# First cross attention: the values product of the second 128 keys as three passes over half-precision splits, with VectorE making the lower split of the turned probabilities

## What is computed

```python
xn = layer_norm(x, g1, b1)                    # context, 257 rows a batch
ln_lat = layer_norm(latents, g2, b2)          # 32 rows a batch
q = ln_lat @ Wq
kv = jnp.concatenate([xn, ln_lat], axis=1) @ Wkv
k, v = jnp.split(kv, 2, axis=-1)              # 16 heads of 64
weight = einsum('bhld,bhnd->bhln', q * scale, k * scale)
weight = softmax(where(full_mask, weight, neg))
out = einsum('bhln,bhnd->bhld', weight, v) @ Wout
```

## Time and profile before

| what | value |
|---|---|
| median of three runs | 2339.83 us |
| the profiled execution's own time | 2338.32 us |
| its span, first to last instruction | 2335.7 us |
| granted TensorE clock, mean of the span | 0.912 |
| PE busy | 1966.3 us, 84% |
| VectorE busy | 1634.2 us, 70% |
| ScalarE busy | 1632.0 us, 70% |
| GpSimd busy | 900.8 us, 39% |

### The profile page before, as it was taken

How to read it: one execution, slowest core, us unless ns; L and a number is a source line. 1 busy time by engine, 2 the same in 40 slices (tenths; PEclk the granted TensorE clock), 3 DMA queues, 4 the chain that set the end, 5 groups by cost and what they waited for, 6 DMA issues and landing times. The chain is left out here.

```text
span 2335.7 us, 56137 instructions
## 1 busy us (share of the span) xinstructions
PE 1966.3 (84%) x15558; PEld 1552.0 (66%) x15558; DVE 1634.2 (70%) x5153; ACT 1632.0 (70%) x4429; POOL 900.8 (39%) x1341
## 2 busy tenths in 40 slices
PE   3799999999999999973430359999999989957997
PEld 3688888888888888851320127777777756625775
DVE  5677777777777777745566738888888878854654
ACT  3588888888888888854365328888888878834553
POOL 2533333333333333303033303333333347733554
PEclk8799999999999999986575669999999999968999
DMA  4211111111111111000000012222222200012322
GB/s 133 68 33 32 32 32 32 32 32 32 32 32 32 32 32 32 19 1 0 0 0 0 0 43 65 66 69 72 63 71 63 67 2 1 1 27 70 93 80 86
DMA packets 124104, 93.87 MB, mean 40 GB/s; under 512 B 14416, under 2 KB 101936, under 8 KB 123904
## 3 DMA queue, kind: packets, MB, share of 16 engines
q1 hardware_dynamic: 122550, 90.88, 14.2%
q10 hardware_dynamic: 1194, 1.58, 0.2%
q0 software_dynamic: 288, 0.56, 0.1%
HBM read 88.26 MB, written 4.72 MB: 40 GB/s over the span
## 5 line engine op out<-in xcount | busy, mean ns | idle before, releaser
L751 ACT ACTIVATE a_prob<-a_neg,a_nmax 128x289 f32<-128x289 f32 x512 | 270.6, 530 | 78.8 <-DVE a_nmax L680 72.9
L1645 ACT ACTIVATE b_prob<-b_neg,b_nmax 128x257 f32<-128x257 f32 x512 | 255.2, 500 | 71.1 <-DVE b_nmax L1592 71.0
L646 POOL TENSOR_TENSOR a_xn<-a_z,g 128x256 f32<-128x256 f32 x128 | 93.2, 728 | 526.3 <-DVE a_z L706 526.3
L808 PE MATMUL a_score<-a_xnT,a_qT 128*128 128x290 f32 x1536 | 274.2, 314 | 1.1 <-DVE a_qT L727 1.1
L836 PE MATMUL a_out<-a_probT,a_xn 128*128 128x256 f32 x1024 | 263.5, 380 | 0.3 <-DVE a_probT L691 0.3
L680 DVE CUSTOM_DVE_ANT_0 a_neg<-a_score,a_bias 128x289 f32<-128x289 f32 x512 | 221.9, 459 | 46.4 <-PE a_score L808 40.7
L808 PEld LDWEIGHTS a_score<-a_xnT,a_qT 128*128 128x128 f32 x1536 | 216.0, 190 | 43.8 <-issue 43.2
L1592 DVE CUSTOM_DVE_ANT_0 b_neg<-b_score,b_bias 128x257 f32<-128x257 f32 x512 | 196.1, 421 | 50.7 <-PE b_score L1688 48.1
L756 ACT ACTIVATE a_prob<-a_prob,a_rinv 128x256 f32<-128x256 f32 x512 | 230.5, 499 | 1.1 <-DVE a_rinv L718 1.0
L836 PEld LDWEIGHTS a_out<-a_probT,a_xn 128*128 128x128 f32 x1024 | 174.8, 191 | 13.7 <-DVE a_probT L691 0.6
L1566 POOL TENSOR_TENSOR b_last_part<-b_v_rows,b_prob 128x128 f32<-128x128 f32 x128 | 52.0, 406 | 317.4 <-ACT b_prob L1645 317.3
(11 more groups left out here) (465 smaller groups left out, 5230.6 us busy)
## 6 DMA issues: line engine op xcount, KB each, us to landing
a_raw<-in_ctx SPq DMA_DIRECT2D x128, 128.0 KB, 3.3
b_raw<-in_ctx SPq DMA_DIRECT2D x128, 128.0 KB, 3.2
m_wide<-expert_weights SPq DMA_DIRECT2D x128, 128.0 KB, 2.9
a_kept<-keep SPq DMA_DIRECT2D x32, 257.0 KB, 3.8
b_kept<-keep SPq DMA_DIRECT2D x32, 257.0 KB, 3.5
b_v_rows<-ctx_tail_values SPq DMA_DIRECT2D x32, 256.0 KB, 3.6
a_tail<-latents_normalised SPq DMA_DIRECT2D x64, 64.0 KB
latents_normalised<-lat_affine SPq DMA_DIRECT2D x8, 256.0 KB, 2.3
```

The costliest lines, as they stand in the source:

```text
L751: nc.scalar.activation(prob[:, par, grp, :], neg[:, grp, :], ACT.Exp, bias=nmax[:, par, grp:grp + 1], scale=-1.0, accum_out=rsum[:, par, g ...
L808: last = nc.tensor.matmul(score_ps[grp % 2][:, 0:even(KEYS0)], qT[:, a, un, bn, 4 * grp:4 * grp + 4, :], xnT[:, c, n, :], start=(p == 0), ...
L1645: nc.scalar.activation(prob[:, n, grp, :], neg[:, par, grp, :], ACT.Exp, bias=nmax[:, par, grp:grp + 1], scale=-1.0, accum_out=rsum[:, n, ...
```

## The change

The second 128 keys' values are taken out of the plain F32 form. `values` is split in `values0` (first 128 keys, as before) and `values1`, which runs three passes of F32R halves for each half of the heads: six F32R instructions of 256 columns where four F32 instructions stood. The halves are made in three places. GpSimd makes those of `xn` (a cast of 128x128 into `xn1[:, n, HI]`, then a subtraction into `xn1[:, n, LO]`). ScalarE's copy L765 writes the upper half of the turned probabilities into `probT1[:, HI, :]` in place of the F32 copy. VectorE subtracts that from the turned probabilities in PSUM and writes `probT1[:, LO, :]`, 128x512 elements, a new instruction between masks 3 and the statistics. TensorE waits for both lower halves ahead of `values1`.

```diff
--- before.py
+++ after.py
@@ -548,6 +548,9 @@
         var, rstd = sb("a_var", [P, 2, 2]), sb("a_rstd", [P, 2, 2])
         z = sb("a_z", [P, 2, 2, D])
         xn = sb("a_xn", [P, 8, 2, D])
+
+        xn1 = sb("a_xn1", [P, 8, 2, D], F32R)
+        probT1 = sb("a_probT1", [P, 2, CH], F32R)
         tail = sb("a_tail", [P, 8, D])
         xnT = sb("a_xnT", [P, 2, 8, even(KEYS0)], F32R)
         kept = sb("a_kept", [P, 2, BPT, N_CTX], BF16)
@@ -575,6 +578,7 @@
         turned, probT_ready = [sem(f"a_turned{n}") for n in range(3)], [sem(f"a_probT_ready{n}") for n in range(3)]
         out_ready, oT_ready, proj_ready, x_added = (sem(f"a_{n}") for n in ("out_ready", "oT_ready", "proj_ready", "x_added"))
         zeroed, tail_prob_ready = sem("a_zeroed"), sem("a_tail_prob_ready")
+        xn1_hi, xn1_ready, probT1_ready = sem("a_xn1_hi"), sem("a_xn1_ready"), sem("a_probT1_ready")
         x_stats_ready = sem("a_x_stats_ready")
         LEAD, LAG = 5, 1
 
@@ -646,6 +650,12 @@
                         nc.gpsimd.tensor_tensor(xn[:, n], z[:, par], spread(k.g1), ALU.mult).then_inc(scaled, 1)
                         pool.wait_ge(scaled, s + 5)
                         nc.gpsimd.tensor_tensor(xn[:, n], xn[:, n], spread(k.b1), ALU.add).then_inc(xn_ready, 1)
+                        pool.wait_ge(xn_ready, s + 5)
+                        if live(g, j, -4):
+                            wait_apart(k, pool, out_ready, s - 3)
+                        nc.gpsimd.tensor_copy(xn1[:, n, HI], xn[:, n, 1]).then_inc(xn1_hi, 1)
+                        pool.wait_ge(xn1_hi, s + 5)
+                        nc.gpsimd.tensor_tensor(xn1[:, n, LO], xn[:, n, 1], xn1[:, n, HI], ALU.subtract).then_inc(xn1_ready, 1)
                     if live(g, j, 5):
                         par = (j + 5) % 2
                         wait_apart(k, pool, mv_ready, s + 6)
@@ -692,6 +702,9 @@
                     if live(g, j, 1):
                         mask(g, j, 2)
                         mask(g, j, 3)
+                    if live(g, j, 0):
+                        dve.wait_ge(probT_ready[1], s + 1)
+                        nc.vector.tensor_tensor(probT1[:, LO, :], turn_ps[1][:], probT1[:, HI, :], ALU.subtract).then_inc(probT1_ready, 1)
                     if live(g, j, 5):
                         n, par = (j + 5) % 8, (j + 5) % 2
                         dve.wait_ge(raw_loaded[n], (g + (j + 5) // 8 + 1) * 16)
@@ -762,7 +775,7 @@
                         exp(g, j, 1)
                     if live(g, j, 0):
                         act.wait_ge(turned[1], s + 1)
-                        nc.scalar.activation(probT[:, 1, :], turn_ps[1][:], ACT.Copy).then_inc(probT_ready[1], 1)
+                        nc.scalar.activation(probT1[:, HI, :], turn_ps[1][:], ACT.Copy).then_inc(probT_ready[1], 1)
                     if live(g, j, 1):
                         exp(g, j, 2)
                         exp(g, j, 3)
@@ -827,14 +840,22 @@
                         last = nc.tensor.transpose(turn_ps[0][:, i * P:(i + 1) * P], prob_tail[:, j % 2, i].rearrange("p f n -> p (f n)"), k.ident[:])
                     last.then_inc(turned[2], 1)
 
-                def values(g, j, kt):
+                def values0(g, j):
                     s = g * 8 + j
-                    pe.wait_ge(probT_ready[kt], s + 1)
-                    if kt == 0:
-                        wait(pe, oT_ready, s)
+                    pe.wait_ge(probT_ready[0], s + 1)
+                    wait(pe, oT_ready, s)
                     for half in range(2):
-                        nc.tensor.matmul(out_ps[:, half, 0:2 * P], xn[:, j, kt, :], probT[:, kt, half * 2 * P:(half + 1) * 2 * P],
-                                         start=(kt == 0), stop=False)
+                        nc.tensor.matmul(out_ps[:, half, 0:2 * P], xn[:, j, 0, :], probT[:, 0, half * 2 * P:(half + 1) * 2 * P],
+                                         start=True, stop=False)
+
+                def values1(g, j):
+                    s = g * 8 + j
+                    pe.wait_ge(xn1_ready, s + 1)
+                    pe.wait_ge(probT1_ready, s + 1)
+                    for a, c in PASSES:
+                        for half in range(2):
+                            nc.tensor.matmul(out_ps[:, half, 0:2 * P], xn1[:, j, a, :], probT1[:, c, half * 2 * P:(half + 1) * 2 * P],
+                                             start=False, stop=False)
 
                 def tail_values(g, j):
                     s = g * 8 + j
@@ -877,7 +898,7 @@
                             last = nc.tensor.matmul(proj_ps, oT[:, h, :], k.U[:, h, :], start=(h == 0), stop=(h == H - 1))
                         last.then_inc(proj_ready, 1)
                     if here:
-                        values(g, j, 0)
+                        values0(g, j)
                         turn_tails(g, j)
                     if live(g, j, 3):
                         n = (j + 3) % 8
@@ -889,7 +910,7 @@
                             last = nc.tensor.transpose(ctx_ps[:, kt * P:(kt + 1) * P], xn[:, n, kt, :], k.ident[:])
                         last.then_inc(ctx_turned, 1)
                     if here:
-                        values(g, j, 1)
+                        values1(g, j)
                         tail_values(g, j)
 
                 run_steps(pe, step, LEAD, LAG)
```

## The result

Four runs of the changed kernel gave 2386.51 to 2390.66 us, with a median of 2388.14; the kernel before gave 2338.88 beside it (four runs, 2337.04 to 2342.24). The ratio is 1.021, with a 95% interval of 1.0192 to 1.0228. The change made the kernel 49 us slower. The forecast was 2393, 54.5 us slower, in a range of 2374 to 2408. The profiled execution took 2386.51 us, its span 2384.7.

What follows compares the result with a forecast made beforehand. A loop through PE, VectorE's reciprocal and ScalarE was taken to bound three of four steps, PE the other. The profiled 2338.32 + 57.3 (subtraction) - 2.8 (shorter product) gave 2392.8, forecast 2393 us, range 2374 to 2408.

Steps and rivals of the forecast that it cites:

- The bound: Of a tile's four steps, one is paced by PE, three by a loop through PE, VectorE's reciprocal and ScalarE.
- The subtraction, 0.61 us in 94 steps: VectorE's new instruction ahead of the reciprocal lengthens the loop in three of four steps: 57.3 us slower.
- The six passes, 0.78 us instead of 0.87: F32R passes on PE replace four F32 instructions, saving 0.09 us in 31 first steps of tiles: 2.8 us gained.
- The sum: Whole kernel: 2338.32 + 57.3 - 2.8 = 2392.8 us, given as 2393.
- What was to cost nothing: ScalarE's copy into F32R, and GpSimd's cast and subtraction of 0.73 us a step, were put at nothing.
- The wait of PE ahead of `tail_values`, put near 1 us: In a tile's second to fourth step PE should wait near 1 us for ScalarE's copy.
- PE as the pace of every step: Rival: VectorE has 0.61 us to spare, only the shorter product counts; 11.4 us less, 2327; chance 0.05.
- That nothing happens: Rival: subtraction slips into VectorE's idle time, shorter product only waits longer on PE; 2338 us; chance 0.04.
- GpSimd against VectorE: Rival: GpSimd's new operations stretch a VectorE instruction on the loop; 9 to 19 us more, 2402 to 2412; chance 0.08.
- The granted clock: Rival: PE's waits lower its clock for a tenth of the stage; up to 94 us more, some 2480; chance 0.05.

Runs made afterwards that it cites:

- e2: Kernel before plus only VectorE's new subtraction, written to a buffer nobody reads, and TensorE's wait for it; 2391.53 us, ratio 1.0231.
- e4: Changed kernel with VectorE's work for later batches moved behind the reciprocal, last keys' scaling and queries' lower half; nothing left out; 2332.62 us, ratio 0.9977 to kernel before.
- e5: Kernel before, F32 products kept, with VectorE's work for later batches moved behind the reciprocal, last keys' scaling and queries' lower half; 2334.56 us, ratio 0.9983.
- e1: Changed kernel without VectorE's new subtraction; its pass reads the upper half again, so six passes remain; 2336.08 us, ratio 0.9988 to kernel before.
- e3: Kernel before plus only GpSimd's new cast and subtraction of 128x128, written to a buffer nobody reads; 2339.29 us, ratio 1.0004.
- e6: Changed kernel with VectorE's subtraction over the first 256 of 512 columns only; other heads' pass reads the upper half; 2362.74 us, ratio 1.0108.

## Why the prediction was right, and where its sizes were off

**The bound.** Right. The loop through PE, VectorE's row up to the reciprocal, ScalarE's scaling and copy, and `tail_values` was read from two distances of 0.04 and 0.06 us. e2 lengthens it by one instruction and pays in full; e4 takes 1.05 us of other work out of it and gets the 0.60 back. What the prediction did not say is that in the kernel before this loop was not the bound alone. The scaling began 514.15 - 513.67 = 0.48 us after the query half, and in e4, where the query half alone holds it, it is 523.87 - 523.39 = 0.48 too. So in this step VectorE's row and ScalarE's own ended together; the fourth step is the same, and only in the third does VectorE's row end last, by 0.1 us (below). That is why 0.61 us more on VectorE's row costs 0.60, while 1.05 us less on it (e5) gives 0.01 in the second and the fourth step.

**The subtraction, 0.61 us in 94 steps.** The mechanism and the price hold: 0.61 from start to start in the timeline, and e1 against the changed kernel gives 7.45 - 6.85 = 0.60 in the second step and 7.04 - 6.44 = 0.60 in the fourth. In the third step it is only 7.03 - 6.52 = 0.51. That step was longer before by 0.09 than the fourth, and the forecast, which read its period from the second step alone, did not see it. In the kernel before the third step's mask 3 starts late, and the scaling begins 520.69 - 520.11 = 0.58 us after the query half (timeline; the third step of the same tile as in the earlier trace rows):

```profile
518.55 0.46 DVE L680 CUSTOM_DVE_ANT_0 a_neg<-a_score,a_bias 128x289 f32<-128x289 f32 x1 [0.21 <-PE a_score L808]
...
518.94 0.08 DVE L680 DVE_READ_ACCUMULATOR2_ANT a_nmax<- 128x1 f32 x1
...
519.07 0.46 DVE L680 CUSTOM_DVE_ANT_0 a_neg<-a_score,a_bias 128x289 f32<-128x289 f32 x1
...
520.11 0.58 ACT L772 ACTIVATE a_qT<-a_q 128x512 fp32r<-128x512 f32 x1
...
520.69 0.91 ACT L756 ACTIVATE a_prob<-a_prob,a_rinv 128x256 f32<-128x256 f32 x2
```

From mask 2 to mask 3 it is 0.52 us here and 0.40 in the second step. The distance is 0.52 and 0.43 by turns from tile to tile; over the third steps of batches 6 to 118 it is 0.49 us in the mean. This delay stands, with the same mean, in the four kernels without the new VectorE instruction (before, e1, e3, e5), and is gone, with 0.40, in the four that have it (the changed kernel, e2, e4, e6), in either order. In e5 it costs nothing, because VectorE's row no longer ends last there. Its cause was not found. It accounts for 31 x 0.09 = 2.8 us of what the forecast was too high, and for e6's miss.

**The six passes, 0.78 us instead of 0.87.** The direction was right, the term too small. From the start of the two context turns to `tail_values` in a tile's first step it was 508.95 - 507.77 = 1.18 us before, with the turns in this row of the same timeline:

```profile
507.77 0.38 PE L889 MATMUL a_ctx<-ident,a_xn 128*128 128x128 f32 x2
```

In the changed kernel it is 532.18 - 531.16 = 1.02 us:

```profile
531.16 0.38 PE L910 MATMUL a_ctx<-ident,a_xn 128*128 128x128 f32 x2
...
531.30 0.95 PE L857 MATMUL a_out<-a_probT,a_xn 128*128 128x256 f32 x6
...
531.36 0.38 ACT L794 ACTIVATE a_probT<-a_turn 128x256 f32<-128x256 f32 x1 [2.27 <-PE a_turn L840]
...
532.18 0.70 PE L868 MATMUL a_out<-a_probT,a_tail 64*128 64x256 f32 x4
```

That is 0.16 us less, and 0.14 by the tiles of e1 against before, where 0.09 was put: 31 x 0.05 = 1.6 us. From the first product to `tail_values` alone it is 508.95 - 507.99 = 0.96 against 532.18 - 531.30 = 0.88, a saving of 0.08, near what was put; the other 0.08 lies between the turns and the first product (0.22 before, 0.14 now), which the forecast did not look at. Its 0.147 us for a pass of 290 columns is also a mean with a longer first distance: the six scores of the earlier trace rows start 0.22 us apart once and 0.13 to 0.14 then. By the Trainium skill ("TensorE: Matmul & The Clock Gate", section "Wait — 56ns, not 53.3ns?") the saving was an estimated 0.21; the trace lies between that and the scaled row.

**The sum.** 94 x 0.61 - 31 x 0.09 was 54.5. With 0.60, with 31 third steps of 0.51, and with 0.14 for the passes it is 94 x 0.60 - 31 x 0.09 - 31 x 0.14 = 49.3 us; measured are 49.3. That the two agree to a tenth is luck: the interval of the ratio is 4 us wide to either side, and in the two profiled executions the copies of batches 0 and 127 lie 47.9 us further apart than before.

**What was to cost nothing.** GpSimd's work did cost nothing (e3), and so did ScalarE's copy into F32R: 0.57 us (L778), as before. The wait of PE ahead of `tail_values`, put near 1 us, is 0.73.

**The rivals.** PE as the pace of every step is refuted by e1 and e2: 20 us less of PE's busy time came with 49 us more, and e1, with the six passes, is back at the time before. That nothing happens is refuted by the result. GpSimd against VectorE is refuted by e3. The granted clock stayed at 1.00 from 200 to 1000 us.

## What to carry to other kernels

Before work is moved to an engine that is "only 70% busy", find in the timeline which of its instructions another engine waits for, and what stands ahead of that instruction in its list: what is put there is paid almost in full (here 0.60 of 0.61 us in two steps of four, 0.51 in a third), and what is taken away from there comes back only until another engine's row ends last. A distance of 0.04 us tells what a longer row will cost; it does not tell what a shorter one will give back, since a second row may end at the same time. A shorter product on the busiest engine gives back only the steps in which that engine really ends last, here one in four. If a list is written by hand, work for later batches belongs behind the instruction that the current batch waits for; that alone turned a loss of 49 us into a gain of 6.

## What the hardware showed that was not expected

The scaling of the last 33 keys (`prob_tail`, 128x132, two SBUF inputs) takes 714 ns in the changed kernel, where GpSimd's gain multiplication starts at about the same time (at 544.81 in the changed kernel's timeline, the scaling at 544.99), and 298 ns in e4, where the order keeps the two apart:

```profile
L733 DVE TENSOR_TENSOR a_prob_tail<-a_prob,a_rinv 128x132 f32<-128x132 f32 x103 | 73.5, 714 | 3.5
...
L740 DVE TENSOR_TENSOR a_qT<-a_q,a_qT 128x512 fp32r<-128x512 f32 x103 | 69.7, 677 | 0.0
```

```profile
L720 DVE TENSOR_TENSOR a_qT<-a_q,a_qT 128x512 fp32r<-128x512 f32 x108 | 74.8, 692 | 0.0
...
L713 DVE TENSOR_TENSOR a_prob_tail<-a_prob,a_rinv 128x132 f32<-128x132 f32 x110 | 32.7, 298 | 3.8
```

The first of these two fences is the changed kernel from 200 to 1000 us (busy us, mean ns of one), the second e4 in the same stretch. The prediction had read the same from the last steps of the kernel before; that a mere change of order frees 0.4 us of VectorE in every step was not foreseen. The queries' lower half, 128x512 with one input in PSUM, is not stretched: it takes 677 ns in the changed kernel, where it starts together with GpSimd's bias addition (both at 545.63 in that timeline), and 692 ns in e4, where GpSimd stood idle beside it in the step shown (from 522.86 to 525.67 us). This agrees with the Trainium skill ("GPSIMD Engine Reference", section "8. Key points"), which names VectorE instructions with two SBUF inputs among those that meet GpSimd at the shared interface.
